# Softmax row sums from folded keys: 128 partitions folded to 64 per head, split, and summed in two full-width float32r passes

## What is computed

```python
q, k, v = (einsum('bsm,hmd->bhsd', x, kernel[n]) for n in range(3))   # B=4, S=1024, D=256, H=16, head size 64
scores = einsum('bhsd,bhtd->bhst', q, k) * (1 / (64 * 64 * 16))
attn = softmax(scores, axis=-1)
out = einsum('bhst,bhtd->bhsd', attn, v)
```

## Time and profile before

| | us |
|---|---|
| median of 3 runs | 1954.52 (1952.67 to 1955.86) |
| the profiled execution | 1952.68 |
| its span | 1950.9 |
| TensorE busy | 1849.5 (95%) |
| VectorE busy | 1354.6 (69%) |
| ScalarE busy | 992.6 (51%) |
| GpSimd busy | 338.4 (17%) |
| mean granted clock of TensorE | 0.979 |

### The profile page before, as it was taken

The page is one execution under the profiler, slowest core; times in us unless marked ns, Lnnn a source line. Parts: engine busy times, 40 slices in busy tenths (PEclk is TensorE's granted clock), DMA queues, the critical chain, the costliest instruction groups (busy, mean ns, idle before and its releaser), DMA issues. The chain is left out here.

```text
span 1950.9 us, 31310 instructions
## 1 busy us (share of the span) xinstructions
PE 1849.5 (95%) x11143; PEld 1180.5 (61%) x11143; DVE 1354.6 (69%) x1737; ACT 992.6 (51%) x1432; POOL 338.4 (17%) x354
## 2 busy tenths in 40 slices
PE   7999999999999999999999999989837999999986
PEld 5445444444444444444444444488827999999982
DVE  5676767677767677767676777866675666666656
ACT  5555454555454555544555445445514555555547
POOL 1000000000000000000000000000005777777764
PEclk9999999999999999999999999999968999999998
DMA  5000000000000000120000000054241334333335
GB/s 167 17 28 17 22 17 28 16 23 17 28 17 22 17 28 17 51 71 28 17 22 17 28 20 15 17 190 176 102 158 34 88 88 86 88 86 86 88 52 173
DMA packets 70077, 110.28 MB, mean 57 GB/s; under 512 B 7627, under 2 KB 45709, under 8 KB 67661
## 3 DMA queue, kind: packets, MB, share of 16 engines
q1 hardware_dynamic: 52861, 85.68, 13.0%
q0 software_dynamic: 17104, 23.12, 6.4%
HBM read 70.20 MB, written 38.57 MB: 56 GB/s over the span
## 5 line engine op out<-in xcount | busy, mean ns | idle before, releaser
L415 ACT ACTIVATE a_e<-banks 128x1024 f32<-128x1024 f32 x512 | 496.5, 1022 | 218.2 <-PE banks L307 218.2
L515 DVE TENSOR_TENSOR a_esum<-a_esum,a_e 128x1024 f32<-128x1024 f32 x384 | 469.5, 1223 | 57.4 <-ACT a_e L415 36.3
L321 PE MATMUL banks<-a_e,a_v 128*64 128x512 f32 x2048 | 495.7, 605 | 0.0
L321 PEld LDWEIGHTS banks<-a_e,a_v 128*64 128x64 f32 x2048 | 124.4, 136 | 238.4 <-issue 175.9
L307 PE MATMUL banks<-a_qh,a_kh 64*128 64x512 f32 x1024 | 230.1, 446 | 5.2 <-issue 5.2
L519 DVE RECIPROCAL a_inv<-banks 128x512 f32<-128x512 f32 x64 | 214.9, 3358 | 15.4 <-PE banks L330 15.4
L512 DVE TENSOR_TENSOR a_esum<-a_e 128x1024 f32<-128x1024 f32 x64 | 78.4, 1226 | 202.5 <-ACT a_e L415 202.5
L61 POOL MEMSET t_ident<- 128x128 f32 x1 | 0.2, 204 | 1245.3 <-POOLq L107 1245.3
L307 PE MATMUL banks<-a_qh,a_kl 64*128 64x512 f32 x1024 | 202.3, 392 | 0.0
L307 PE MATMUL banks<-a_ql,a_kh 64*128 64x512 f32 x1024 | 201.8, 391 | 0.0
L1622 ACT ACTIVATE e_g<-banks,e_b1c 128x256 f32<-128x256 f32 x280 | 116.0, 469 | 143.6 <-PE banks L1569 142.9
(11 more groups left out here) (233 smaller groups left out, 3196.3 us busy)
## 6 DMA issues: line engine op xcount, KB each, us to landing
attn_out<-a_ot SPq DMA_DIRECT2D x64, 256.0 KB, 2.0
a_w<-w_qkv SPq DMA_DIRECT2D x32, 256.0 KB, 3.1
raw<-attn_out SPq DMA_DIRECT2D x4, 2048.0 KB, 8.9
t_ot<-attn_out SPq DMA_DIRECT2D x4, 2048.0 KB, 8.7
raw<-w_up SPq DMA_DIRECT2D x8, 1024.0 KB, 5.0
raw<-w_down SPq DMA_DIRECT2D x8, 1024.0 KB, 7.4
raw<-x_t SPq DMA_DIRECT2D x8, 512.0 KB, 9.3
acc_rows<-shared SPq DMA_DIRECT2D x4, 1024.0 KB, 8.9
```

The costliest lines, as they stand in the source:

```text
L321: mm = pe.matmul(o_acc[slot % 2][h * DH:(h + 1) * DH, :], v[quad % 2][:, n, head], e[n % NE][:, h * BANK:(h + 1) * BANK], start=n == 0, st ...
L415: act.activation(e[n % NE], ring[n % 2], ACT.Exp, scale=SCALE).then_inc(e_ok, 1)
L515: dve.tensor_tensor(acc[:, :], acc[:, :], e[n % NE], ALU.add).then_inc(add_ok, 1)
```

## The change

The 128 partial sums of each query are folded to 64 before the matmul. ScalarE copies, for each head, the half of `esum` that lies on the other head's partitions to this head's 64 partitions (`halves`); VectorE adds it to the half that already lies there (`folded`: head 0 on partitions 0 to 63, head 1 on 64 to 127). ScalarE rounds it to float32r (`folded_h`), VectorE takes the rest (`folded_l`), and two float32r matmuls with a 128x128 matrix of two blocks of ones sum both heads at once. The sums of a slot move on TensorE from step 0 of the next slot to behind its first unit (step 1). On VectorE `fold` stands ahead of the slot's first add, `fold_low` in step 1, and `normalize` moves from step 0 to behind the unit of step 2. On ScalarE `halve` stands between the exponentials 0 and 1, `fold_high` between 2 and 3. Some semaphores of the other branch, which doesn't run, share those of this one. GpSimd builds the block matrix at the start.

```diff
             def sums(slot):
-                pe.wait_ge(add_ok, slot * ADDS + ADDS)
+                pe.wait_ge(fold_lo, slot + 1)
                 if slot:
                     pe.wait_ge(inv_ok, slot)
-                for h in range(2):
-                    mm = pe.matmul(sum_ps[h * DH:(h + 1) * DH, :], ones[:, :], esum[slot % 2][:, h * BANK:(h + 1) * BANK],
-                                   start=True, stop=True)
-                mm.then_inc(sum_done, 1)
+                pe.matmul(sum_ps, blocks_r[:, :], folded_h[:, :], start=True, stop=False)
+                pe.matmul(sum_ps, blocks_r[:, :], folded_l[:, :], start=False, stop=True).then_inc(sum_done, 1)
...
                         values(slot, 2 * j - 1)
                         if len(todo) >= j:
                             pe_unit(pe, todo[j - 1])
+                        if j == 1 and slot:
+                            sums(slot - 1)
                     elif slot:
                         values(slot - 1, ST - 2)
                         values(slot - 1, ST - 1)
-                        sums(slot - 1)
...
+            def halve(slot):
+
+                act.wait_ge(add_ok, slot * ADDS + ADDS)
+                if slot:
+                    act.wait_ge(fold_ok, 2 * slot)
+                for h in range(2):
+                    act.copy(halves[h * DH:(h + 1) * DH, :], esum[slot % 2][(1 - h) * DH:(2 - h) * DH, h * BANK:(h + 1) * BANK])\
+                       .then_inc(half_ok, 1)
+
+            def fold_high(slot):
+                act.wait_ge(fold_ok, 2 * slot + 2)
+                if slot:
+                    act.wait_ge(sum_done, slot)
+                act.copy(folded_h[:, :], folded[:, :]).then_inc(fold_hi, 1)
...
                     probs(slot, 2 * j)
+                    if j == 0 and slot:
+                        halve(slot - 1)
+                    if j == 1 and slot:
+                        fold_high(slot - 1)
                     probs(slot, 2 * j + 1)
...
             dve.tensor_copy(ones_r[:, :], ones_f).then_inc(ones_r_ok, 1)
+            dve.wait_ge(blocks_ok, 3)
+            dve.tensor_copy(blocks_r[:, :], blocks_f)
...
-                        dve.wait_ge(sum_done, slot - 1)
+                        dve.wait_ge(fold_ok, 2 * slot - 2)
...
+            def fold(slot):
+
+                if slot:
+                    dve.wait_ge(fold_hi, slot)
+                    dve.wait_ge(fold_lo, slot)
+                for h in range(2):
+                    rows = slice(h * DH, (h + 1) * DH)
+                    dve.wait_ge(half_ok, 2 * slot + h + 1)
+                    dve.tensor_tensor(folded[rows, :], esum[slot % 2][rows, h * BANK:(h + 1) * BANK], halves[rows, :], ALU.add)\
+                       .then_inc(fold_ok, 1)
+
+            def fold_low(slot):
+                dve.wait_ge(fold_hi, slot + 1)
+                dve.tensor_tensor(folded_l[:, :], folded[:, :], folded_h[:, :].bitcast(F32), ALU.subtract).then_inc(fold_lo, 1)
...
                 for j in range(ST // 2):
                     if j:
                         add(slot, 2 * j)
+                    elif slot:
+                        fold(slot - 1)
+                    if j == 1 and slot:
+                        fold_low(slot - 1)
                     add(slot, 2 * j + 1)
                     if j and len(todo) >= j:
                         dve_evacuate(dve, todo[j - 1])
-                    if j == 0 and slot:
+                    if j == 2 and slot:
                         normalize(slot - 1)
...
+            fold(SLOTS - 1)
+            fold_low(SLOTS - 1)
             normalize(SLOTS - 1)
```

More of the change, by code:

```diff
@@ L128, in attention @@
         esum = [sb(f"a_esum{u}", [P, S]) for u in range(2)]
+        halves = sb("a_halves", [P, BANK])
+        folded, folded_h, folded_l = sb("a_folded", [P, BANK]), sb("a_folded_h", [P, BANK], R32), sb("a_folded_l", [P, BANK], R32)
+        blocks_r = sb("a_blocks_r", [P, P], R32)
         inv = sb("a_inv", [P, BANK])
@@ L146, in attention @@
         wtop, xtop, b1, b2, b3, flag_f = (inv[0:1, 192 + n:193 + n] for n in range(6))
-        ones_f = inv[:, 256:256 + P]
+        ones_f, blocks_f = inv[:, 256:256 + P], inv[:, 384:384 + P]
         x_in = [sem(f"a_x_in{j}") for j in range(KD * T // S)]
@@ L159, in attention @@
             sem("a_" + n) for n in ("s_done", "e_ok", "add_ok", "pv_done", "sum_done", "inv_ok", "o_ok"))
+        half_ok, fold_ok, fold_hi, fold_lo, blocks_ok = (
+            sem("a_" + n) for n in ("half_ok", "fold_ok", "fold_hi", "fold_lo", "blocks_ok"))
         ot_out = keep["ot_out"]
@@ L428, in act_bounded @@
                         act_rows_high(act, 2 * (i // PAIRS + 1) + i % PAIRS - 1)
+            halve(SLOTS - 1)
+            fold_high(SLOTS - 1)
         def dve_rows_low(dve, j):
@@ L555, in attention @@
         g_v_ready = sem("a_g_v_ready")
-        g_s_done = sem("a_g_s_done")
-        g_top_ok = sem("a_g_top_ok")
+        g_s_done = s_done
+        g_top_ok = sum_done
         g_shift_ok = sem("a_g_shift_ok")
-        g_e_done = sem("a_g_e_done")
-        g_inv_ok = sem("a_g_inv_ok")
-        g_e_norm = sem("a_g_e_norm")
+        g_e_done = e_ok
+        g_inv_ok = inv_ok
+        g_e_norm = add_ok
         g_et_done = sem("a_g_et_done")
         g_et_evac = sem("a_g_et_evac")
-        g_pv_done = sem("a_g_pv_done")
-        g_o_evac = sem("a_g_o_evac")
+        g_pv_done = pv_done
+        g_o_evac = o_ok
         g_ot_out = sem("a_g_ot_out")
@@ L708, in _ @@
             gp.memset(ones_f, 1.0).then_inc(ones_ok, 1)
+            gp.wait_ge(ones_ok, 2)
+            gp.memset(blocks_f, 0.0).then_inc(blocks_ok, 1)
+            for h in range(2):
+                gp.wait_ge(blocks_ok, h + 1)
+                gp.memset(blocks_f[h * DH:(h + 1) * DH, h * DH:(h + 1) * DH], 1.0).then_inc(blocks_ok, 1)
+            gp.wait_ge(blocks_ok, 3)
             make_identity(gp, ident, ident_ok)
```

## The result

The changed kernel is slower: median 2027.18 us (2025.36 to 2036.68) against 1954.66, ratio 1.038, 95% interval 1.0366 to 1.0399. The direction and the mechanism (a ring of waits through all three engines) were those of the prediction. The size, +72.5 us, was not: 52.0 had been forecast and the range ended at 2024.

The account below looks back on a forecast made before the run. The prediction took attention to run at TensorE's pace before the change, and a 19.90 us loop of waits after it. Its terms, 24.3 + 6.8 - 0.4 + 10.6 + 2.6 + 5.1 + 3.0 = +52.0 us, gave 2006 us, range 1976 to 2024.

Parts of the forecast that it names:

- TensorE's own gain: Sums on TensorE: two float32r passes, 0.46 us, replace 0.85 a slot; 19.05 us a slot if nothing else is late.
- The ring: Once-a-slot loop from scores of tile 3 through second unit, evacuation, normalize, last adds, copies and exponential: 19.90 us.
- To ScalarE: Last part of the loop, from last add through two copies at 0.52 and the exponential to TensorE: 2.16 us.
- rival 3: TensorE's granted clock falls because it stops each slot, some 1.9 us a slot: 2121 us; chance 0.03.
- the sum for slots 56 to 61: Attention slots without a value unit: stay at 19.89 us against 17.86 before, +10.6 us in all.
- six rows splits: VectorE's activation-row splits in six slots, covered before, now stand in the loop: 6 x 1.14 = +6.8 us.
- slot 62: Attention slot without units: 17.2 to 17.4 us against 14.7 before, +2.6 us.
- from the last add to the next stage: After the last slot, copies, fold, high and low parts and sums are hidden by nothing: +3.0 us.
- the start: Slot 1 of attention runs before the loop of waits binds: -0.4 us.
- 10.6 + 2.6 + 5.1: Late attention terms in us: slots 56 to 61, then slot 62, then slot 63 up to its last add.
- Rival 1: TensorE stays the bound of attention, without gaps, at 19.05 us a slot: 1937 us; chance 0.08.
- Rival 2: ScalarE's half copies cost by partitions, a step of 0.30 us: loop 19.46, time 1981 us; chance 0.07.

Follow-up runs that it names:

- e4_matmuls_alone: Changed kernel without half copies and folding; the new sum matmuls multiply constant tiles of ones: 1939.26 us, ratio 0.9927.
- e2_copies_behind: Changed kernel with the half copies behind the exponential of tile 1 and fold behind the slot's first add; normalize stays in step 2: 1940.31 us, ratio 0.9931.
- e9_filler_half: Changed kernel plus 12 unread 128-column matmuls in each of the six slots without a value unit: 2022.67 us, ratio 1.0354.
- e1_norm_step1: Changed kernel with normalize in step 1, behind the first unit, in place of step 2: 1956.18 us, ratio 1.0016.
- e3_norm_alone: Kernel before the change with only normalize moved from step 0 to step 2; no fold, no new matmuls: 1968.30 us, ratio 1.0078.
- e5_same_rows: Changed kernel with both half copies reading and writing partitions 0 to 63, so no exchange of partitions: 2009.79 us, ratio 1.0291.
- e8_third_copy: Changed kernel plus one more 64x512 ScalarE copy into a spare tile behind each slot's two: 2068.30 us, ratio 1.0592.
- e6_filler: Changed kernel plus 24 unread 128-column matmuls in each of the six slots without a value unit: 2027.37 us, ratio 1.0386.

## Why the prediction was right and wrong

**TensorE's own gain** was right: 0.46 for 0.85. The period of 19.04 against a forecast 19.05 is shown by e4_matmuls_alone and reached with all the work done in e2_copies_behind.

**The ring** was right link by link but one. From the start of scores 3 to the end of the second unit: 717.91 + 0.39 - 708.38 = 9.92 (9.93 forecast). From there to the end of the last add, with both evacuations and normalize: 703.44 + 2.54 for one slot, 726.09 for the next, so 726.09 - 718.30 = 7.79 for 1.26 + 4.00 + 2.55 = 7.81. From the last add to scores 3: 708.38 - 705.98 = 2.40 for 2.16, and here alone the walk is off. TensorE's stop ahead of scores 3: 0.79 (0.85). The step that failed is the copies' step in "To ScalarE": "Two copies 2 x 0.52". It is 0.64, outside the bounds of 0.30 and 0.60 that I gave, because the row used was of instructions that all start at partition 0. I had even cited the Trainium skill ("VectorE: DVE Perf Modes", section "Two Vector instructions with no wait between them") for VectorE, that such a start takes away the overlap, and set it aside as sitting beside the wait; I did not ask whether ScalarE does the same. With it, the period is 20.11 and not 19.90: 0.21 x 61 = **12.8 us**.

**The clock** was rival 3, with a chance of 0.03 and the price of a fall in every slot. What came is a fall in a few: 2.9 + 1.6 + 2.9 + 1.6 = **9.0 us** in this execution. The step that failed is the sum for slots 56 to 61: "so they stay at 19.89" gives the time but not the stop. The missing unit leaves TensorE idle 1.6 us longer, 2.4 in all. I weighed the clock with the plain slot's 0.85 alone; after those stops it never fell, after stops of 1.7 us and more it did at times. The evidence that I set against the rival was also misread. The 0.55 us at 39.97 is idle time of the weight loads; TensorE's passes did not stop there, the one before ended only at 39.48 + 0.66 = 40.14:

```profile
39.48 0.66 PE L307 MATMUL banks<-a_qh,a_kl 64*128 64x512 f32 x2
39.97 0.80 PE L307 MATMUL banks<-a_qh,a_kh 64*128 64x512 f32 x2
```

So it said nothing of what a stop does. That the falls belong to the long stops is shown by e9_filler_half (none in six late slots with stops of 0.9 us, where four of six fell at 2.4) and by the counts in the last section; why a given stop ends in a fall and the next, equally long, does not, stays open.

**Together**: 52.0 + 12.8 + 9.0 = 73.8 of 75.6 at the end of the stage. Of the other terms, six rows splits cost 1.13 each (1.14 forecast), slot 62 17.33 - 14.68 = 2.65 (2.6, though with the longer copies), and from the last add to the next stage it is now 1344.97 - 1335.17 = 9.8 where it was 6.1: 3.7 for the forecast 3.0. Two terms were off by about 2 us each and cancel, which is luck: the first adds of slot 2 stand at 80.39 and 78.35, so the start cost 2.0 us where -0.4 was forecast, and from the first add of slot 56 to the last add it is 26.8 us longer, which without the falls (9.0) and the copies (1.3) is 16.5 where 10.6 + 2.6 + 5.1 = 18.3 was forecast.

**The cause** as I named it, that the move of normalize takes the cover from the copies, is shown from both sides: e1_norm_step1 gives the cover back, e2_copies_behind takes away the need for it, and e3_norm_alone shows that without copies the late normalize costs 15 us, mainly in the late slots. Rival 1 lost by order, not by volume: the same operations run at 19.04.

**The range** was too narrow above: it took in the ring's lags but counted the clock only as a rare catastrophe, so that two moderate errors of the same sign left it.

## What to carry to other kernels

When work is added to engines with spare time, walk the loop that goes through all of them once a period, not their totals: here the same instructions gave 2027 or 1940 us, depending on whether two copies, and the fold that waits for them, stood ahead of or behind one exponential and one add. Put an added wait behind the work that the bound engine needs next. And give each forecast stop its length in every kind of slot, since the longest ones can also cost clock.

## What the runs showed of the hardware

- ScalarE loses its overlap where the start partition changes. Two copies of 64x512 that exchange partitions 0 and 64 and the instruction behind them step by 0.64 us, so without overlap (a copy takes 0.62); with the same partitions they step by 0.52 (e5_same_rows). After a copy that reads from 64 but writes from 0, an exponential that reads the matmul banks and writes from 0 still overlaps (0.52, e8_third_copy). That points to the output's start as what counts there; for the input alone no run decides it.
- VectorE does likewise: the two folds, 0.69 each, take 1.40 together, a step of 0.71 where 0.61 is usual. The trace agrees with the Trainium skill ("VectorE: DVE Perf Modes", section "Two Vector instructions with no wait between them"), by which such an instruction starts only when the earlier ones have ended. It cost nothing here, as forecast.
- A copy of half the partitions takes 0.617 us, as a full one does (0.63 in the earlier trace rows). Rival 2 falls.
- TensorE's granted clock fell after some stops and not after others of the same length, and the more often, the longer the stop. The table counts the stops between 45 us and the last add in the profiled executions of the changed kernel, e5_same_rows, e6_filler, e8_third_copy and e9_filler_half. Afterwards passes stepped by 0.43 in place of 0.23 (the 1.2 GHz level) for up to 6 us, and a fall cost 1.2 to 1.7 us or, in three slots, 2.9.

| stop, us | stops | falls |
|---|---|---|
| 0.5 to 1.3 | 251 | 0 |
| 1.7 | 6 | 1 |
| 1.9 | 19 | 6 |
| 2.1 | 9 | 5 |
| 2.4 | 12 | 7 |
| 2.6 to 2.9 | 7 | 7 |

- A float32r pass of 128 columns with a fresh 128x128 weight load each steps by 0.12 us and not by a quarter of a 512-column pass (0.06).
